# SyncE's queue in two attention layers: the transposed maxima's rows are issued ahead of the next pair's first slots, on even steps

## The reference, cut to what matters

```
x = x + attention0(layernorm(x), ctx)        # 16 heads of 8, rotary positions, no mask
x = x + ffn0(layernorm(x))                   # 128 -> 512 -> 128, quantized weights, relu
x = x + attention1(layernorm(x), ctx, mask)  # 16 query heads of 8, 4 key heads, mask, norm of the output
x = x + ffn1(layernorm(x))                   # 8 experts, each token goes to one
attention: softmax(Q K^T / sqrt(8)) V per head, then the output projection
```

## Time and profile before

| | us |
|---|---|
| median of 3 runs | 530.79 (529.56 to 532.43) |
| the profiled execution, its own time | 530.89 |
| its span in the profile | 529.1 |
| layer 0's attention, steps under way on all engines | about 28 to 180 |
| layer 1's attention | about 240 to 418 |

### The profile page before, as it was taken

One profiled execution on the slowest core, in us unless ns is written; L12 is line 12 of the kernel. 1 busy time (PEld: TensorE's weight loads), 2 busy tenths in 40 slices (PEclk: granted clock), 3 DMA queues, 4 the chain that ended last, 5 costly groups with the idle time before them and its releaser, 6 DMA issues.

```text
span 529.1 us, 19004 instructions
## 1 busy us (share of the span) xinstructions
PE 453.4 (86%) x6103; PEld 348.9 (66%) x6103; DVE 377.4 (71%) x1113; ACT 348.2 (66%) x892; POOL 336.8 (64%) x710
## 2 busy tenths in 40 slices
PE   2688899999987888998799999999988615999992
PEld 2456677777765777997456666566655405999991
DVE  6787887888888557864567888898987562555551
ACT  4356788888876455664267788788875714666660
POOL 5787987788763346766444674888887670555552
PEclk9788999999999999999789999999998956999996
DMA  7556455555551720453222232243331133444430
GB/s 180 144 138 157 116 143 129 139 130 144 132 123 43 242 45 1 78 118 92 59 53 61 75 75 70 78 109 100 95 83 60 64 121 92 108 107 107 106 99 21
DMA packets 99108, 53.43 MB, mean 101 GB/s; under 512 B 25235, under 2 KB 96035, under 8 KB 99027
## 3 DMA queue, kind: packets, MB, share of 16 engines
q1 hardware_dynamic: 95666, 45.06, 34.6%
q0 software_dynamic: 2784, 6.82, 3.7%
q10 hardware_dynamic: 576, 0.53, 0.4%
HBM read 17.89 MB, written 8.81 MB: 50 GB/s over the span
## 4 chain that ended last, share of the span: by engine, by line
PE 62%; DVE 10%; DMA 9%; issue 6%; POOL 6%; SPq 3%; ACT 2%; ACTq 0%; DVEq 0%; POOLq 0%
PE bank L738 10%; PE bank L965 6%; PE score L686 6%; PE scoreT L955 4%; DMA stack<-negpT 4%; PE bank L873 4%; DVE negmax L1603 4%; PE scoreT L863 3%; DMA stack<-pieces 3%; PE score L651 3%; PE bank L787 3%; PE bank L600 3%; PE score L955 2%; PE scoreT L661 2%; PE scoreT L713 2%
## 5 line engine op out<-in xcount | busy, mean ns | idle before, releaser
L1603 DVE TENSOR_REDUCE negmax<-score 128x8 f32<-128x1024 f32 x128 | 156.3, 1221 | 46.2 <-PE score L686 45.2
L1077 ACT ACTIVATE P<-scoreT 128x1024 f32<-128x1024 f32 x128 | 131.2, 1025 | 48.2 <-PE scoreT L704 26.6
L738 PE MATMUL bank<-P,Vc 128*32 128x128 f32 x2048 | 71.7, 282 | 1.3 <-issue 0.8
L1517 POOL DMA_INDIRECT out<-by x39 | 37.4, 960 | 48.2 <-DVE by L1963 47.2
L738 PEld LDWEIGHTS bank<-P,Vc 128*32 128x32 f32 x2048 | 53.8, 112 | 15.5 <-issue 12.1
L686 PE MATMUL score<-stack 64*128 64x128 bf16 x896 | 45.8, 223 | 8.6 <-DMA stack<-pieces 4.3
L686 PEld LDWEIGHTS score<-stack 64*128 64x128 bf16 x896 | 26.1, 96 | 38.7 <-issue 22.1
L1358 POOL TENSOR_TENSOR negp<-negmax,blank 128x16 bf16<-128x16 f32 x64 | 14.1, 220 | 55.5 <-DVE negmax L1603 53.9
L965 PE MATMUL bank<-M,P 128*128 x312 | 41.4, 276 | 0.5 <-DVE by L1963 0.5
L1250 ACT ACTIVATE P<-scoreT,We 128x128 f32<-128x128 f32 x104 | 29.7, 369 | 15.3 <-PE scoreT L955 15.3
L965 PEld LDWEIGHTS bank<-M,P 128*128 128x128 f32 x312 | 38.0, 192 | 0.7 <-issue 0.7
(11 more groups left out here) (220 smaller groups left out, 1210.2 us busy)
## 6 DMA issues: line engine op xcount, KB each, us to landing
stack<-pieces SPq DMA_DIRECT2D x96, 128.0 KB, 2.6
stack<-pieces SPq DMA_DIRECT2D x96, 64.0 KB
XB<-expert_rows SPq DMA_DIRECT2D x39, 66.0 KB, 1.9
XA<-expert_rows SPq DMA_DIRECT2D x39, 64.0 KB, 1.9
XR<-in_x SPq DMA_DIRECT2D x4, 512.0 KB, 4.7
ctxT<-in_ctxT SPq DMA_DIRECT2D x16, 128.0 KB, 2.3
stack<-blank SPq DMA_DIRECT2D x32, 64.0 KB, 2.2
stack<-negpT SPq DMA_DIRECT2D x64, 32.0 KB, 1.9
```

The costliest lines, as they stand in the source:

```text
L738: mm = nc.tensor.matmul(PVOUT[VCOL * i:VCOL * (i + 1), half * 128:(half + 1) * 128], Vc[:, k % BODY, at:at + VCOL], P32[:, 2 * p_slot(L, k ...
L1077: nc.scalar.activation(P32[:, at:at + 2, :], SCORET[:], ACT.Exp, scale=SCALE).then_inc(sem("exp_done"), 1)
L1517: nc.gpsimd.indirect_dma_start(out=out, out_offset=bass.IndirectOffsetOnAxis(ap=at_, axis=0), in_=by[r][:, 0:D], in_offset=None).then_inc( ...
L1603: nc.vector.tensor_reduce(negmax[:, k % 2, :, half * HQ:(half + 1) * HQ], SCORE[:].rearrange("p r (h k) -> p r h k", h=HQ), AX.X, ALU.max, ...
```

## The change

On even steps of both layers `max_rows(t + 1, j + 1)` moves from behind `stack_first(j + 4)` to ahead of it. On odd steps the order stays as it was. Nothing is added or removed, and no other engine's program changes.

```diff
                 def step(t, j):
                     if j % 2 == 0:
                         blank_max(j + 4)
+                        max_rows(t + 1, j + 1)
                         stack_first(j + 4)
                     else:
                         stack_last(j + 3)
-                    max_rows(t + 1, j + 1)
+                        max_rows(t + 1, j + 1)
                     if j % 2 == 1:
                         if L == 0:
                             load_ctx(j + 7)
```

## The result

| | before | after |
|---|---|---|
| median, us | 530.17 (526.87 to 532.43, 4 runs) | 541.62 (540.29 to 542.46, 4 runs) |
| ratio, 95% interval | | 1.0207 (1.0172 to 1.0243) |
| the profiled execution, its own time | 530.89 | 540.29 |
| its span | 529.1 | 538.5 |

The change makes the kernel 2.1% slower, some 11 us by the ratio and 9.4 us between the two profiled executions. I had forecast 3.4 us, with a range that ended at 538.5.

The account below looks back on a forecast made before the run. PE was taken to bound the kernel, nearly always busy in steady stretches, so every new wait counts. Layer 0's +4.3 less layer 1's 0.9 gave +3.4 us on 530.89: 534.3, range 530.2 to 538.5.

Parts of the forecast that it names:

- The mechanism: Layer 0, steady period: rows issued at the same moment, last slots 1.4 us later against 1.2 to 1.3 us of slack.
- The account of layer 0: Layer 0: losses of 1.0, 1.2, 0.8, 0.9 and 0.4 summed to 4.3 us, between 0.8 and 9.6.
- Landings behind instruction packets: Layer 0, pairs at 86.91, 147.98 and near 69: later slots mostly meet the packet's tail; 0.9 us lost, 0 to 3.9.
- Rival 3: Jams carried along and odd rows waiting behind slots: losses 8.5 less gains 0.9, giving 538.5 us; chance 0.17.
- The start: Layer 0, pairs at 37.75 and 50.02, loads ahead of the last slots: 1.2 and 0.8 us lost.
- my bound of 1.4: Layer 0, pair at 50.02 with F1 and F2 between: 0.8 us lost, range 0.3 to 1.4.
- Steady pairs: Layer 0, six pairs between 91 and 143: PE waits about 0.17 us each, 1.0 us lost, 0 to 1.8.
- The other pairs and the rows of layer 0: Layer 0: pairs near 82 and 160 lose 0.4 us (0 to 1.1); even rows PE waited for win 0.2 in all.
- Layer 1: Layer 1: rows no longer held behind first slots, 0.9 us gained (0 to 2.5); later slots cost nothing, at most 0.3.

Follow-up runs that it names:

- the run of steps 0 and 2: Rows ahead of the first slots on steps 0 and 2 of layer 0 alone, against the kernel before: 1.0068 (1.0025 to 1.0111), 3.6 us slower.
- layer 1 alone: Rows ahead of the first slots on even steps of layer 1 only, against the kernel before: 1.0014 (0.9977 to 1.005).

## Why the prediction was wrong, point by point

**The mechanism was right.** Rows issued at the same moment, slots 1.4 us late (predicted 1.4 for the start of the last four; at their end 1.46), plain transit of 2.4, a wait of 0.17 us at PE in the period shown: each stands in the rows after. The odd rows come 0.5 to 0.7 late instead of fitting just so, with no wait of their own. The direction was right too. The size was not: the sum was 3.4 us and the kernel lost 9 to 11.

**The account of layer 0.** PE's waits for SP's DMAs there grew by 7.5 us: two pairs at the start +3.5, three pairs that met instruction packets +3.3, six steady pairs +1.2, two more pairs +1.1, and the waits for rows -1.6. I had 2.0, 0.9, 1.0, 0.4 and -0.2: the packets' term was off the most. The layer became 8.3 us longer, and not by these waits alone. PE's busy time in it rose by 2.9 us, from 132.34 to 135.21, with the same instructions at a lower clock (below), and its idle time by 5.4, since its other waits shrank.

**Landings behind instruction packets: 0.9, measured about 3.3, of the upper end's 3.9.** This is the step that failed most clearly: "Slots issued 1.4 us later mostly meet its tail, and land not 1.4 but some 0.3 us later". They do not meet the tail. At 92.97 and 156.96 the landings still took 3.62 and 3.76 us, against 3.98 and 4.11, and in 156.8 to 160.8 the instruction queue again shows its packet:

```profile
q8 instruction: 1, 0.02, 2.2%
q14 instruction: 1, 0.01, 0.8%
```

PE waited 2.15 us there, after 1.12 before, and 1.34 for the one of 92.97, after 0.41. (The 0.41 is a low value: three other traces with layer 0 as before have 0.76 to 0.92 at this place.) The third pair, near 75, waits 1.30 where it did not wait before. Its last landing has plain length, 2.43; what came late there was SP:

```profile
70.76 4.96 SPq L440 DMA_DIRECT2D stack<-pieces  x6
```

Six slots took 4.96 us instead of 3.95, since one issue at 71.4 lasted 1.50, and q8's packet starts between 71.5 and 71.75. Together 1.03 + 0.93 + 1.30 = 3.3. The packets moved with the work: q8's start at about 88.3 and 149.3 in the trace before and at about 93.8 and 156.8 after, 5.5 and 7.5 us later, where the slots that they meet are issued 6.1 and 9.0 later. So a late slot meets its packet again. The Trainium skill, "DMA: Bandwidth & Descriptors", section "Queues, rings and completion order", has the engine go round-robin between its rows by packets; no run here shows that order itself, but what I drew from it, that a packet stays where it was in time, does not follow and was wrong here. And the slack was doing a second job that I counted for one rival only: 1.25 us of it swallowed part of each such delay in pairs that otherwise did not wait at all. Rival 3 said this, at 0.17, and gave 538.5; it was the nearest.

**The start: 2.0, measured 3.6** (interval 1.3 to 5.9, the run of steps 0 and 2). PE's two waits grew from 2.01 and 0.75 us to 3.75 and 1.78 in that run, and to 3.54 and 2.74 with the whole change. In the latter, at step 2's pair, the time from the end of ACT's copy to the last slot's landing was 8.0 us before and 9.8 after (45.97 to 54.00; 46.40 to 56.23): 1.8 us, above my bound of 1.4.

Behind this second wait PE's clock fell to 1.2 GHz for 3.4 us in the changed kernel. I read the clock only in the stretches where it was full, and had no term for it. Lower clock is part of what these two traces differ by: besides this stretch the changed kernel has one at 29.6 to 33.0, and the two can make up most of the 2.9 us of busy time. That the waits of PE cause it is not shown. Of the five traces with the start shifted four have such a stretch near 57, and none of the six others; but the fifth is that of the run of steps 0 and 2, whose clock is full from 49 to 191 and whose layer 0 still ends at 175.23, 2.7 to 4.1 us later than in the four kernels with layer 0 as before. A stretch of the same length at 43.3 to 46.7 stands in the trace before, and in none of the five other traces whose start is the same.

**Steady pairs: 1.0, measured 1.8.** Six periods took 51.97 us before (ACT's copies that end at 93.43 and 145.40) and take 53.80 after (99.19 and 152.99). The waits for slots that the profile shows were sized right: 0.27, 0.16, 0.17, 0.32, 0.29 and under 0.15, some 1.2 to 1.3 together. What I had not counted is that PE's groups overlap in the profile, where their ends are modelled, when none waits. The group ahead of the pair's first score, before and after:

```profile
116.18 1.03 PE L600 MATMUL bank<-xnT,W 128*128 128x256 f32 x4
```

```profile
122.51 1.03 PE L601 MATMUL bank<-xnT,W 128*128 128x256 f32 x4
```

Before, the score starts at 117.14, 0.07 us ahead of the end at 117.21; after, at 123.71, 0.17 behind the end at 123.54. The profile counts 0.17, the start is 0.24 later, and over six pairs that is 0.4 us. The last 0.1 is in one pair: from `scoresT` to `pv` it is 0.43 us at 123.94, in the five others 0.31 to 0.33. The trace before has 0.43 once too, at 91.26; why is open.

**The other pairs and the rows of layer 0: 0.4 and -0.2, measured 1.1 and -1.6.** The waits at 86.59 and 169.79 are 0.21 and 0.92. PE's waits for rows at 36.74, 77.66 and 157.02, 0.90, 0.39 and 0.50 us before, are gone but for 0.22. I had put them at 0.1 each. These rows too went out at once in the kernel before (at 33.22, 74.93 and 154.42, all within 0.03 us of the copy), so what they won is in their landing or in PE's coming later; the runs do not tell which.

**Layer 1: -0.9, measured +0.7** (-1.2 to +2.7). I "put nothing" for the slots, because no slot landing was on the chain and the slots are half as large. Neither was a slack. SP's time for a slot is the same, 0.59 us for 64 KB as 0.61 for 128, so the shift is too. SP's queue and PE in the changed kernel:

```profile
303.73 0.53 SPq L461 DMA_DIRECT2D stack<-negpT  x1
304.47 4.28 SPq L442 DMA_DIRECT2D stack<-pieces  x6
309.03 0.53 SPq L461 DMA_DIRECT2D stack<-negpT  x1
...
311.00 0.37 PE L652 MATMUL score<-XR,negI 64*64 64x512 bf16 x1 [0.65 <-DMA stack<-pieces]
```

ACT's copy is done at 303.71, the slots end only at 308.75, and PE waits. The traces show the loss more clearly than the time does: from the first copy of layer 1 to the last it is 157.3 us with the whole change and 157.0 with layer 1 alone, and 155.5 to 156.6 in the six other kernels whose layer 1 is as before. The trace before is the exception with 158.1; it has a stretch of half clock at 405.1 to 408.5, where none of the others has one.

**The clock between the layers: no term, 1.7 in the profiled execution.** The 3.4 us at 196.9 lie in the feed-forward part, which the change does not touch. Nothing ties them to the change: the traces of the three other kernels with layer 0 as before have such a stretch there too (at 187, 209 and 249), and of the seven with a changed layer 0 two have none.

## What to carry to other kernels

In a queue that issues in order, an instruction that waits sets the time of everything behind it. Before moving one forward, write down for each DMA behind it how late it may be, at the reader, in every stretch where the code runs and not only in the steady one; if the rows already leave the moment they are ready, there is little to win (here 1.6 us in layer 0) and that slack to spend. A slack that looks unused is what absorbs late landings: price a shift against the worst landing of the trace, not against the median.

## What the runs showed of the hardware that was not expected

A DMA of 32 KB with nothing of SP's just ahead of it took 3.84 us to land instead of 1.8 to 2.0 while two instruction packets, 24 KB in all, went by. An issue of SP can be long when a packet goes by: 1.50 us for a slot at 71.4 and 1.51 for rows at 93.72, each less than 0.4 us ahead of a packet's start, instead of 0.6 and 0.54. The issue of a DMA holds ACT's queue for 0.55 us, as it does SP's, and ACT sat idle for 0.68 us before its next copy. And a wait that the profile shows at PE counts from the end of the group before, while without a wait the next group starts 0.07 us ahead of that end. Stretches of half clock of 3.4 us come and go between traces of kernels that are the same up to that point: a difference of 1.7 us between two single traces can be one of these.
